# Moving two VectorE products of an attention stage to GpSimd, with a sum taken over by TensorE

## The reference

```python
x = x + 0.5 * ffn(layernorm(x))        # 8 experts, 128 -> 512 -> 128, one expert a token (argmax)
x = x + attn(layernorm(x))
x = x + 0.5 * ffn(layernorm(x))

def attn(x):                            # 16 heads of 8 features, chunks of 128 tokens
    q, k, v = silu(x @ Wq), silu(x @ Wk), silu(x @ Wv)
    # a chunk, for each head:  scores = (q @ k.T) * mask,  mask[i, j] = exp(-s * (i - j)) for i >= j
    #   o  = scores @ v + lam_q * (q @ kv)            lam_q[i] = exp(-s * (i + 1))
    #   kv = lam_c * kv + (k * lam_k).T @ v           carried to the next chunk
    o = (o - mean(o)) * rsqrt(var(o) + eps) * gamma + beta
    gate = sigmoid(x @ Wg1 @ Wg2)
    return o * gate @ Wo
```

## Time and profile before

| | |
|---|---|
| median of 3 runs | 503.57 us (501.15 to 504.87) |
| profiled execution | 504.27 us |
| its span, first to last instruction | 502.5 us |
| mean granted TensorE clock | 0.849 of full |
| busy: PE, VectorE, GpSimd, ScalarE | 376.0, 347.6, 301.8, 192.8 us |
| instructions on VectorE, GpSimd | 1064, 386 |

### The profile page before, as it was taken

One profiled execution on the slowest core, in us unless ns is written; L12 is line 12 of the kernel. 1 busy time (PEld: TensorE's weight loads), 2 busy tenths in 40 slices (PEclk: granted clock), 3 DMA queues, 4 the chain that ended last, 5 costly groups with the idle time before them and its releaser, 6 DMA issues.

```text
span 502.5 us, 10537 instructions
## 1 busy us (share of the span) xinstructions
PE 376.0 (75%) x2474; PEld 331.9 (66%) x2474; DVE 347.6 (69%) x1064; ACT 192.8 (38%) x590; POOL 301.8 (60%) x386
## 2 busy tenths in 40 slices
PE   5693796699999859586797988372899720699983
PEld 2592796599988746465676776262798610699983
DVE  4937473178876796999989879994776700377861
ACT  1360452145546322336355352401565200255541
POOL 1047988856651796877847676765050378466564
PEclk9555798589999997999988979695699965699998
DMA  8982774257681008500000000012544321266630
GB/s 246 283 310 81 219 222 149 80 149 206 200 250 53 16 12 231 146 0 0 2 1 1 1 2 0 0 48 65 167 144 139 118 80 49 83 188 195 203 122 6
DMA packets 54218, 56.08 MB, mean 112 GB/s; under 512 B 6828, under 2 KB 39881, under 8 KB 53904
## 3 DMA queue, kind: packets, MB, share of 16 engines
q1 hardware_dynamic: 48736, 45.85, 31.8%
q0 software_dynamic: 4992, 8.94, 5.0%
q10 hardware_dynamic: 432, 0.63, 0.4%
HBM read 39.69 MB, written 17.53 MB: 114 GB/s over the span
## 4 chain that ended last, share of the span: by engine, by line
PE 26%; issue 25%; DVE 19%; POOL 15%; SPq 5%; another core or an unknown queue 4%; DMA 1%; ACT 1%; DVEq 1%; POOLq 1%; ACTq 0%
PE bank L1061 9%; PE bank L1071 9%; POOL out_x L396 7%; POOL scratch L372 3%; POOL slots_in L385 3%; DVE o_in L879 3%; PE bank L1153 2%; DVE st L666 2%; DVE qS L870 2%; PE bank L1119 2%; SPq L288 1%; PE bank L1025 1%; SPq L298 1%; POOL x L396 1%
## 5 line engine op out<-in xcount | busy, mean ns | idle before, releaser
L1061 PE MATMUL bank<-slot_xT,w_ring 128*128 128x128 f32 x736 | 110.0, 293 | 19.0 <-issue 8.6
L1061 PEld LDWEIGHTS bank<-slot_xT,w_ring 128*128 128x128 f32 x736 | 98.7, 206 | 23.8 <-issue 18.1
L385 POOL DMA_INDIRECT slots_in<-rows,slot_of x64 | 62.0, 969 | 67.1 <-DVE slot_of L792 51.3
L833 DVE TENSOR_SCALAR hT_b<-bank,b_cur 128x128 f32<-128x128 f32 x184 | 55.7, 344 | 40.3 <-remote 24.9
L1071 PE MATMUL bank<-w_sb,hT_a 128*128 x368 | 62.0, 293 | 23.1 <-issue 18.4
L1119 PE MATMUL bank<-outer_all,decay_sb 128*128 128x256 f32 x256 | 71.2, 405 | 10.4 <-POOL outer_all L277 6.8
L277 POOL TENSOR_TENSOR outer_all<-qkv 128x512 f32<-128x512 f32 x60 | 63.3, 1084 | 12.6 <-ACT qkv L562 12.5
L524 ACT ACTIVATE hT_a<-bank,b_cur 128x128 f32<-128x128 f32 x184 | 57.5, 364 | 31.5 <-remote 15.3
L1071 PEld LDWEIGHTS bank<-w_sb,hT_a 128*128 128x128 f32 x368 | 50.8, 200 | 27.7 <-issue 27.5
L1119 PEld LDWEIGHTS bank<-outer_all,decay_sb 128*128 128x128 f32 x256 | 49.4, 203 | 27.7 <-issue 8.1
L372 POOL MEMSET scratch<- 128x256 f32 (+1 forms) x112 | 40.3, 360 | 42.7 <-DVE ring L840 33.6
(11 more groups left out here) (119 smaller groups left out, 562.3 us busy)
## 6 DMA issues: line engine op xcount, KB each, us to landing
w_ring<-in_w1t SPq DMA_DIRECT2D x92, 256.0 KB
ring<-slots_in SPq DMA_DIRECT2D x92, 72.0 KB
slots_in<-fill SPq DMA_DIRECT2D x2, 1656.0 KB, 13.0
rows<-in_x SPq DMA_DIRECT2D x8, 256.0 KB, 6.2
w_sb<-in_w2t SPq DMA_DIRECT2D x1, 2048.0 KB
rows<-x SPq DMA_DIRECT2D x8, 256.0 KB, 4.9
slots_in<-fill SPq DMA_DIRECT2D x1, 1944.0 KB, 15.1
slots_in<-fill SPq DMA_DIRECT2D x1, 1368.0 KB, 8.7
```

What stands on the lines that cost most here:

```text
L385: pool.indirect_dma_start(slots_in[u], bass.IndirectOffsetOnAxis(ap=slot_of[u][:, t:t + 1], axis=0), row_of(unit.first + t), None).then_in ...
L833: last = nc.vector.tensor_scalar(hT_b[G % 2][:, f * P:(f + 1) * P], bank_b[:, f * P:(f + 1) * P], b1_cur[G % 2][:, 2 + f:3 + f], 0.0, ALU. ...
L1061: last = mm(to[:, f * P:(f + 1) * P], w1_ring[G % W1_BUFS][:, (2 * half + f) * P:(2 * half + f + 1) * P], slot_xT[G % 2][:, :], start=True ...
```

## The change

The decayed queries and the gate product leave VectorE.

- Queries: ScalarE now copies the transposed queries from PSUM into `qdT` (`copy_qT`, semaphore `qT_copied`), and GpSimd multiplies them in place by `decay_q` (`decay_queries`), in the turn that uses them, between `half_sum(n, 2)` and `decay_keys`.
- Gate: GpSimd forms t * o_nT at the end of its turn, for chunks 0 to 5; chunks 6 and 7 stay on VectorE in the same plain form. The missing 1 * o_nT is added on PE: `out_product` accumulates `o_nT @ Wo` and `o_gT @ Wo`, so it has eight matmuls and no longer four.
- `out_product` now stands after state product 1 of its turn, and no longer after state product 0. `o_nT` may be written again only when the output product has read it, so `output_copy` waits for `wo_ready` in place of `gated`.

```diff
+            def decay_queries(n):
+                pool.wait_ge(qT_copied, n + 1)
+                pool.tensor_tensor(per_batch(qdT[n % 2][:, :]), per_batch(qdT[n % 2][:, :]),
+                                   cst("decay_q").unsqueeze(1).to_broadcast([P, BATCH, P]), ALU.mult).then_inc(qdT_done, 1)
+            def gate(s):
+                pool.wait_ge(onT_copied, s.n + 1)
+                pool.wait_ge(gate_done, s.n + 1)
+                wait(pool, wo_ready, s.n)
+                pool.tensor_tensor(o_gT[:, :], gateT[s.par][:, :], o_nT[:, :], ALU.mult).then_inc(gated, 1)
...
                 half_sum(n, 2)
+                decay_queries(n)
                 if n + 1 < STEPS:
                     decay_keys(n)
...
                 outer_part(n + 1, 0, 3)
+                if 0 < n < STEPS - 1:
+                    gate(step(n - 1))
...
+            def copy_qT(s):
+                act.wait_ge(qT_ready, s.n + 1)
+                wait(act, inter_ready, s.n - 1)
+                nc.scalar.activation(qdT[s.par][:, :], bank[5][:, :], ACT.Copy).then_inc(qT_copied, 1)
...
             def output_copy(k):
                 act.wait_ge(onT_ready, k)
-                wait(act, gated, k - 1)
+                wait(act, wo_ready, k - 1)
...
                     gate_tanh(step(k))
+                    if k + 1 < STEPS:
+                        copy_qT(step(k + 1))
...
-            def front(s):
-
-                dve.wait_ge(qT_ready, s.n + 1)
-                wait(dve, inter_ready, s.n - 1)
-                nc.vector.tensor_tensor(per_batch(qdT[s.par][:, :]), per_batch(bank[5][:, :]),
-                                        cst("decay_q").unsqueeze(1).to_broadcast([P, BATCH, P]),
-                                        ALU.mult).then_inc(qdT_done, 1)
...
-                nc.vector.scalar_tensor_tensor(out=o_gT[:, :], in0=gateT[s.par][:, :], scalar=1.0, in1=o_nT[:, :],
-                                               op0=ALU.add, op1=ALU.mult).then_inc(gated, 1)
+                nc.vector.tensor_tensor(o_gT[:, :], gateT[s.par][:, :], o_nT[:, :], ALU.mult).then_inc(gated, 1)
...
-                if k + 1 < STEPS:
-                    front(step(k + 1))
                 if 0 <= k:
                     join(here)
-                if 0 <= k - 1:
+                if k == STEPS - 1:
                     gate(step(k - 1))
...
                 for b in range(BATCH):
-                    last = mm(bank[7][:, b * D:(b + 1) * D], o_gT[:, b * P:(b + 1) * P], wo_sb[:, :], start=True, stop=True)
+
+                    mm(bank[7][:, b * D:(b + 1) * D], o_nT[:, b * P:(b + 1) * P], wo_sb[:, :], start=True, stop=False)
+                    last = mm(bank[7][:, b * D:(b + 1) * D], o_gT[:, b * P:(b + 1) * P], wo_sb[:, :], start=False, stop=True)
...
-                    if h == 0 and 0 <= k - 2 < STEPS:
+                    if h == 1 and 0 <= k - 2 < STEPS:
                         out_product(step(k - 2))
```

More of the change, by code:

```diff
@@ L245, in build @@
         first_outer_done, table_loaded = sem("first_outer_done"), sem("table_loaded")
+        qT_copied = sem("qT_copied")
         halved = sem("halved")
@@ L650, in _ @@
             expert_pass(0, {42: lambda: first_ahead(0), 43: copy_first_xn, 44: lambda: first_qkv(0), 45: lambda: first_qkv(2)})
+            copy_qT(step(0))
             first_ahead(1)
@@ L991, in _ @@
             expert_pass(0, {38: first_stats, 39: chain_at(0, 4), 40: chain_at(4, 8), 41: chain_at(8, SMALL + 1),
-                            46: lambda: (first_outer(), front(step(0)))})
+                            46: first_outer})
             for k in TURNS:
@@ L1087, in norm_transpose @@
                 pe.wait_ge(xn_done, BATCH * (s.n + 1))
-                wait(pe, qdT_done, s.n)
+                wait(pe, qT_copied, s.n)
                 transpose4(bank[5], lambda b: xn[:, b * D:(b + 1) * D], xnT_ready)
@@ L1227, in _ @@
                 if k == ROUTE_TURN:
-                    pe.wait_ge(qdT_done, k + 2)
+                    pe.wait_ge(qT_copied, k + 2)
                     route_counts(2)
```

## The result

| | before | after |
|---|---|---|
| median of 4 runs, same chip | 504.22 us (501.15 to 506.77) | 517.47 us (511.74 to 519.62) |
| profiled execution, its span | 504.27, 502.5 us | 517.74, 515.9 us |
| mean granted TensorE clock | 0.849 | 0.843 |
| busy: PE, VectorE, GpSimd, ScalarE | 376.0, 347.6, 301.8, 192.8 us | 388.2, 345.1, 319.0, 197.0 us |

The changed kernel is slower: ratio 1.0228 (95% interval 1.0118 to 1.0337); whether by more than 2% this pair does not settle. The forecast was 510.9, slower, range 503 to 518: the direction and the mechanism came as forecast, the size did not. The change cost 13.25 us where 7.3 were forecast, and the time stands only half a microsecond inside the range. All ratios here leave out runs over 1.5% above the fastest of the same kernel (one of the changed kernel's four, 519.62 us; one run of e7 at 1206.79), while the medians hold every run.

The account below looks back on a forecast made before the run. A latency loop from shift to residual, nearly as long as VectorE's work, was taken to bound the turn. Terms 0.9 + 0.9 + 0.9 + 0.6 + 1.2 + 1.9 + 0.9 = +7.3 gave 510.9 us, range 503 to 518.

Parts of the forecast that it names:

- turn 0: GpSimd's queries' product in turn 0 delays the scatters and so turn 1, with no cover: +0.9 us.
- product side, turns 2 and 3: At full clock the doubled, later output product starts the residual at 215.70, not 215.26: +0.44 a turn, +0.9 us.
- product side, turns 4 to 6: The doubled, reordered output product delays the residual at the low clock: 0.3 us a turn, +0.9 us for three.
- VectorE held, five turns: More GpSimd products hold small VectorE instructions: 0.1 us a turn (0 to 0.6), forecast as +0.6 for six turns.
- routing: Between turns 6 and 7 GpSimd's longer run of products holds the routing chain's small steps: +1.2 us, -1.2 without holds.
- late products: Doubled output products of steps 6 and 7 delay the second expert layer on PE: +1.9 and +0.9 us.
- The loop, not VectorE, ends the turn: The latency loop from shift to residual decides; VectorE's saved 1.56 us a turn becomes idle time before the residual.
- The rival in which VectorE sets the pace: Six turn boundaries save 1.56 us each, so the kernel gets faster: 496.7 us; chance 0.15.
- GpSimd as the pace: Rival: gate and its wait make outer products late for state products in five turns, 6.0 us more: 517; chance 0.1.
- turns 2 and 3, at full clock: These two turns were taken to run at 2.4 GHz, each 0.44 us longer.
- turns 4 to 6 begin at 1.2 GHz: These three turns were taken to start at the low clock, each 0.3 us longer.
- the clock is kinder: Rival: turns 4 to 6 begin at full clock, 507.0 us, or routing is not held, 508.5; chance 0.23.

Follow-up runs that it names:

- e7: e2 with the output product behind state product 0, queries of chunks 0 and 7 on VectorE, residual ahead of the second query product: 498.02 us, 1.0015 of before.
- e4: Changed kernel with the decayed queries of chunks 0 and 7 back on VectorE: 507.93 us, 1.0131 of before.
- e3: Kernel before with only the doubled output product, behind state product 1; plain gate product and queries on VectorE, nothing added to GpSimd: 508.84 us, 1.0162 of before.
- e2: Changed kernel with 1 + t formed on ScalarE and four output matmuls again; queries and gate stay on GpSimd: 500.73 us, 1.0029 of before.
- e5: Changed kernel run once more without any edit, beside other runs of the kernel before: 513.17 us, 1.0286 of before.
- e6: Kernel before with only its single output product of four matmuls moved behind state product 1: 500.21 us, 1.0013 of before.
- e8: Kernel before with only VectorE's residual and its statistics put ahead of the second query product: 497.87 us, 0.9977 of before.
- e1: Changed kernel with the doubled output product back in its old place, behind state product 0: 512.35 us, 1.021 of before.
- e11: e7 with GpSimd's outer products of the second half ahead of half sum 0: 496.92 us, 0.9948 of before.
- e12: Kernel before with only GpSimd's last two outer products of the second half ahead of half sum 0: 501.03 us, 1.001 of before.
- e10: e9 with the decayed queries of chunks 1 to 6 on GpSimd and ScalarE, gate and output product as before: 499.38 us, 1.0012 of before.
- e9: e8 with GpSimd's last two outer products of the second half ahead of half sum 0: 498.33 us, 0.997 of before.

## Why the prediction was right, point by point

| step | forecast | first profile | the runs |
|---|---|---|---|
| turn 0 | +0.9 | +1.3 to turn 2 | e4: 0.97 is the query product |
| product side, turns 2 and 3 | +0.44 each | +2.49, +0.33 | e3, full clock: +0.33 |
| product side, turns 4 to 6 | +0.3 each | -0.13, +1.81, +0.23 | clock |
| VectorE held, five turns | +0.5 | +1.10 | e2: +0.48 a turn |
| routing | +1.2 | +1.36 | e5: +1.37 |
| late products | +2.8 | +2.65 | five doubled against nine: +2.15 |
| start, end | 0 | -0.32, +2.6 | the same code |

**The loop, not VectorE, ends the turn: right.** The loop is the way from `shift` over `o_nT`, `xn`, PE's queue and the output product to the residual. All the marks named for it came: over 1 us idle in front of the residual in turns 2 to 6, 20.86 at full clock (forecast 20.78), turn 1's statistics 0.8 later, 1.1 counted from attention's start. The rival in which VectorE sets the pace (496.7) is out; e3 shows the loop's length with VectorE's work untouched. That a saving on VectorE gives nothing while nothing is added to PE is shown by e2. GpSimd as the pace is out too: its gate was 1.6 early, and PE's idle time in front of state products for which outer products came late grew only from 6.8 to 8.2 us in the whole span.

**The hold: right in kind, low in size.** From residual to `shift` the changed kernel took 0.16 to 0.35 a turn more than the kernel before, for the 0.1 taken. With the doubled product the residual comes so late that `mean` misses the outer products (0.18 in turns 2 to 6); as soon as the residual is earlier, the hold takes what the loop gives (e2, e6, e7, e8). The prediction treats the small instructions as held here and there. With an earlier residual they are a third limit: the outer products end 9.4 to 9.7 after `shift`, and 10.7 us of VectorE's work follow `mean` (e6: 237.61 to 248.28), 20.1 to 20.4 together. In before VectorE's work (19.76 busy), the loop (20.34) and this hold (20.3) are that close together. The Trainium skill (GPSIMD Engine Reference, Key points) speaks of contention between the two engines over SBUF; the rows agree and show its form here: an instruction of 12 columns lasts 0.50, 0.75, 0.88 or 1.11 instead of 0.17, to the end of the GpSimd product beside it.

**Routing: right,** +1.36 for +1.2 (+1.90 in e1 and e2), and by the cause named: GpSimd's products ran to 12.8 after `shift` (forecast 12.7), `upto` took 1.37 beside them for 0.42. e4 ties 0.4 of it to the queries; the rest is argued from these rows.

**What failed is the step "turns 2 and 3, at full clock" and "turns 4 to 6 begin at 1.2 GHz".** I took the pattern of one profile for a property of the kernel. I also read that pattern coarsely: turns 4 to 6 of the kernel before begin at full clock, and the granted clock is 0.50 for some 3.5 us in turns 4 and 5 and for 6.8 only in turn 6, the one I showed and took the 0.3 from. In the changed kernel's first profile it is 0.50 for 6.8 us in turns 2, 5 and 6, for 3.5 in turn 4, and never in turn 3. From `shift` to residual:

| turn | 2 | 3 | 4 | 5 | 6 |
|---|---|---|---|---|---|
| before | 7.86 | 7.88 | 9.13 | 8.77 | 10.42 |
| after | 10.35 | 8.19 | 9.00 | 10.58 | 10.65 |
| e5 | 10.26 | 10.65 | 9.30 | 10.65 | 10.65 |
| e3 | 8.66 | 8.19 | 9.43 | 10.64 | 9.10 |

At full clock it is 8.19 for 7.86, forecast 8.30. In turn 6, where both ran low, it is 10.65 for 10.42, inside the 0.2 to 0.4 forecast. The term that was mis-sized is how many turns run low, and for how long: turns 2 and 5 alone bring 4.3 us of the 5.8 in the five turns, where 2.3 were forecast for all five. The rival "the clock is kinder" had this with the wrong sign; its counterpart, the clock unkinder, had no case of its own. The 2.6 us at the end are within the scatter of that part, which is the same code everywhere. That the time still fell inside the range is in part luck: the range was widened for other terms, and no term in it stands for more low turns.

**Does the doubled product bring the low clock about?** The table speaks for a cost, not for a cause. Its five kernels took 111.1 on average for the five turns, the nine others 104.2, while full clock accounts for 0.3 to 1.0 of the difference in each turn (20.67, 20.86 and 21.36 for 20.34 and less). The rest goes with low turns being longer there: up to 23.3 and 23.6 (e1, at a mean of 0.86), in e6 to e11 22.1 at most (e6, 0.85). But e12 and before, without it, had a turn of 22.8 and 22.9 too, and the mean clock (0.87 to 0.94 with, 0.89 to 1.00 without) doesn't part them. At the same mean of 0.89 the changed kernel took 112.2, e12 108.0 and e8 105.2. That more PE work between `xn` and residual goes with dearer low turns is borne out by these sums, one profile each; that it makes low turns more frequent is not shown. The excess of the five turns over the forecast is so put down to the clock by the rows of these profiles, not by an experiment that set the clock.

## What to carry to other kernels

An engine that is busy 97% of a turn need not be its pace. Follow the boundary from its last event to the next, add the loop of waits, and look for a third limit as long as the first two, such as a small instruction held by a neighbour's run of products. Work taken from the busy engine is a gain only if nothing is put on that loop; here eight passes more a turn on PE cost 1.6% (e3), and the two products moved were worth nothing (e2). Where the clock falls in a different turn of each execution, give the low turns a case of their own, with count and price, both ways.

## What the runs showed of the hardware

- The granted clock at the same place of the same kernel changes from one execution to the next: turn 3 of the changed kernel at 1.00 in one profile, at 0.50 from 232 to 238 in another. A turn then takes 23.3 in place of 20.9. In e2 all five turns stayed at 1.00 (20.24 to 20.27), and its time was still that of before.
- VectorE's busy time contains the time for which GpSimd holds it: e10's VectorE does 0.60 less a turn than e9's and is busy 19.63 for 19.68 us.
- Between the row scatters of the second layer's first group and the join of turn 7 VectorE stands still with no releaser that the trace names. In the changed kernel:

```profile
350.47 3.04 DVE L895 TENSOR_REDUCE o_in<-qS 128x64 f32<-128x512 f32 x3
358.94 0.69 DVE L905 TENSOR_TENSOR o_all<-bank,o_in 128x512 f32<-128x512 f32 x1 [5.43 <-remote]
```

  The wait ends 3.65 after the last of the sixteen scatters starts (355.29), in the kernel before 3.83 after it (347.10, join at 350.93), and 3.5 to 3.7 after it in ten of the twelve variants. In e3 and e5 it is another instruction that stands, and it goes on 2.3 and 2.7 after the last scatter's start. So the end of turn 7 mostly follows `slot_of`, though not by one fixed delay. What it waits for wasn't tried and stays open.
